# A two-layer graph kernel on one core: the first layer's product re-associated as A (x W0), its adjacency sums run in eight column passes, and each tile's norm and projections placed inside later tiles' sums

## The reference, cut to what matters

```python
# layer 0
a_hat = adjacency + eye;  dinv = rsqrt(deg)              # deg = max(row count of adj, 1)
a_norm = dinv * a_hat * dinv                             # [4096,1] factors: both scale rows
x1 = layernorm(x + relu((a_norm @ x + x) @ W0 + b0))
# layer 1, on x1
attn_a = sigmoid(concat[adj @ x1, x1] @ Wa.T + ba);      attn_b likewise with Wb, bb
h = x1 @ W_sa;  s_left = h @ a_l;  s_right = h @ a_r
e = where(adj != 0, exp(-leaky_relu(s_left[:, None] + s_right[None, :], 0.01)), 0)
x_a = (e / (e.sum(1) + 1e-5)) @ h
x_b = adj @ (x1 @ W_gcnb) + b_gcnb
out = layernorm(x1 + sigmoid(attn_a * x_a + attn_b * x_b))
```

## Time and profile before

| | |
|---|---|
| three runs | 918.81 us median, 917.81 to 919.22 |
| profiled execution, its span | 917.2 us, first to last instruction |
| PE busy, modelled | 887.0 us, 97% |
| DVE, ACT, POOL busy | 640.8, 461.9, 49.3 us |
| transfers | 121.49 MB, 132 GB/s over the span |

### The profile page before, as it was taken

One profiled execution on the slowest core, in us unless ns is written; L12 is line 12 of the kernel. 1 busy time (PEld: TensorE's weight loads), 2 busy tenths in 40 slices (PEclk: granted clock), 3 DMA queues, 4 the chain that ended last, 5 costly groups with the idle time before them and its releaser, 6 DMA issues.

```text
span 917.2 us, 18143 instructions
## 1 busy us (share of the span) xinstructions
PE 887.0 (97%) x6815; PEld 676.6 (74%) x6815; DVE 640.8 (70%) x1347; ACT 461.9 (50%) x652; POOL 49.3 (5%) x106
## 2 busy tenths in 40 slices
PE   3999999999999999997999999999999999999996
PEld 2444444444688788886888888888888888888885
DVE  5988810021599988869978768777786797797762
ACT  2400026665399966634745545554554564465350
POOL 0000000010122310000000000000000000000000
PEclk9999999999999999998999999999999999999998
DMA  9999959998613211020211110120120120110000
GB/s 337 422 416 416 417 210 396 330 388 339 253 47 128 75 36 53 1 75 13 75 65 31 56 63 17 58 74 11 63 74 11 63 74 11 63 54 32 13 24 12
DMA packets 44701, 121.49 MB, mean 132 GB/s; under 512 B 5456, under 2 KB 33136, under 8 KB 33520
## 3 DMA queue, kind: packets, MB, share of 16 engines
q1 hardware_dynamic: 44656, 120.89, 34.7%
HBM read 95.69 MB, written 25.18 MB: 132 GB/s over the span
## 4 chain that ended last, share of the span: by engine, by line
PE 77%; DVE 15%; issue 4%; ACT 3%; DMA 1%; POOL 0%; DVEq 0%; SPq 0%; POOLq 0%; ACTq 0%
PE ps L1067 33%; PE ps L924 24%; PE ps L1016 19%; DVE ec L788 3%; DVE ps L712 1%; DVE em L797 1%; DVE xs L717 1%; DVE fb L686 1%; DMA xs<-in_x_dram 1%; ACT ec L487 1%; DVE lnst L724 1%; DVE x1t L693 1%; ACT em L490 1%; DVE acct L675 1%; DVE sc L566 1%
## 5 line engine op out<-in xcount | busy, mean ns | idle before, releaser
L1067 PE MATMUL ps<-fb,em 128*128 128x257 f16 x3072 | 345.3, 275 | 6.4 <-DVE em L797 6.4
L1067 PEld LDWEIGHTS ps<-fb,em 128*128 128x128 f16 x3072 | 300.8, 98 | 48.7 <-issue 6.9
L1016 PE MATMUL ps<-fa,pan 128*128 128x258 f16 x2048 | 231.9, 273 | 0.0
L924 PE MATMUL ps<-res,y 128*128 128x512 fp8e4 x1024 | 222.0, 379 | 1.5 <-DVE y L633 0.8
L1016 PEld LDWEIGHTS ps<-fa,pan 128*128 128x128 fp8e4 x2048 | 199.3, 97 | 29.6
L788 DVE SCALAR_TENSOR_TENSOR ec<-slb,sr,pan 128x256 f32<-128x256 f32 x512 | 207.9, 479 | 7.7 <-issue 7.5
L487 ACT ACTIVATE ec<-ec,sc 128x2048 f32<-128x2048 f32 x64 | 127.9, 1999 | 133.6 <-DVE ec L788 133.6
L924 PEld LDWEIGHTS ps<-res,y 128*128 128x128 f16 x1024 | 100.0, 98 | 121.7 <-issue 1.2
L797 DVE SCALAR_TENSOR_TENSOR em<-ec,em 128x2048 f16<-128x2048 f32 x64 | 146.4, 2288 | 16.9 <-ACT em L490 16.9
L490 ACT ACTIVATE em<-ec 128x2048 f16<-128x2048 f32 x64 | 122.3, 1911 | 7.5
L414 ACT ACTIVATE res<-strip 128x2048 uint8<-128x2048 f32 x32 | 61.1, 1913 | 106.2 <-DMA strip<-in_adj_dram 106.2
(11 more groups left out here) (103 smaller groups left out, 477.6 us busy)
## 6 DMA issues: line engine op xcount, KB each, us to landing
strip<-in_adj_dram SPq DMA_DIRECT2D x63, 1024.0 KB, 9.8
a_scratch<-res SPq DMA_DIRECT2D x16, 1024.0 KB, 12.0
pan<-a_scratch SPq DMA_DIRECT2D x16, 1024.0 KB, 5.0
x_scratch<-xs SPq DMA_DIRECT2D x32, 128.0 KB, 1.7
x1r<-x_scratch SPq DMA_DIRECT2D x32, 128.0 KB, 2.1
out_dram<-ot SPq DMA_DIRECT2D x32, 128.0 KB, 1.7
xs<-in_x_dram SPq DMA_DIRECT2D x3, 1024.0 KB, 8.4
slb<-sl_scratch SPq DMA_DIRECT2D x16, 128.0 KB, 4.7
```

What stands on the lines that cost most here:

```text
L924: return pe.matmul(ps[:, sum_bank(g, dh), :], y[:, jb, part, dh * P:(dh + 1) * P], res[:, 2 * (g % NG2):2 * (g % NG2) + 2, jb, :].bitcast(F8),
L1016: mm = pe.matmul(PA(m)[:, 0:GC], pan[:, slot, jb, (m % 2) * P:(m % 2 + 1) * P].bitcast(F8), fa[:, jb, part, :], start=(jb == 0 and part == 0),
L1067: mm = pe.matmul(PH(m)[:, 0:HC], em[slot][:, e_part, jb, (m % 2) * P:(m % 2 + 1) * P], fb[:, jb, h_part, :], start=(jb == 0 and e_part + h ...
```

## The change

Layer 0 is `A (x W0)` in place of `(A x) W0`. By tile, in the order of the program:

- A first loop transposes each x tile on PE (`xt_step`), copies it out on ACT, multiplies it by W0 (`z_step`) and copies the result to `zf` on DVE (L613). `y` is now made of `zf`; its scale comes from a bound, the maximum of x times the largest absolute column sum of W0 (`z_bound`, `z_scale`). A column of ones in y gives the row count.
- The adjacency is read in 128 strips of four row tiles x 256 columns (1 KB contiguous in DRAM), ring of six, and cast by DVE (L600, a plain tensor_scalar) and ACT in turns, without accumulators. A pass covers two panels, q and q + 8, that is four row tiles (`PT = 4`). Codes of three passes are held in SBUF; each pass's codes go to DRAM when cast.
- `sum_rows` (L1031): the codes are stationary, 257 columns of y move, the result is untransposed, one bank a tile, and no bank is copied out. W0 is already in it.
- The first pass's rows are interleaved with the x W0 loop, 12 tiles behind. From the fifth tile on, a tile's 64 matmuls are cut in four quarters; after the first and third come `t_step` and `p_step` of the tile two before.
- DVE's per-tile work (`degree`, `residual`, `stats`, together `head`), ACT's normalize and copies, POOL's power and a new POOL add (z + bias, `zb`) follow. PE may not start tile n before the statistics of tile n - 4 are done (bank reuse).
- x1 goes to DRAM from ACT's queue, through a ring of four. The remaining steps, projections, A and E tiles, epilogue, are as before; panels are taken in the order q, q + 8.

```diff
-            for jb in range(T):
-                act.activation(y[:, jb, 0, :], xs[:, jb, :], ACT.Copy, scale=sc[:, SX]).then_inc(S["yhi_ready"], 1)
...
-            def sums(jb, dh, part, g):
-                return pe.matmul(ps[:, sum_bank(g, dh), :], y[:, jb, part, dh * P:(dh + 1) * P],
-                                 res[:, 2 * (g % NG2):2 * (g % NG2) + 2, jb, :].bitcast(F8),
...
+            z_bound()
+            for c in range(4):
+                x_max(c)
+            for t in range(T):
+                z_copy(t)
+                if t in (1, 3):
+                    x_max(4 + t // 2)
+                if t == 4:
...
+                if t == 5:
+                    z_scale()
+                if t >= YLAG:
+                    y_lo(t - YLAG)
+                if 9 <= t < 25 and t % 2 == 1:
+                    cast(1)
+                if t == 22:
+                    weight_columns()
+                if t == 26:
+                    weight_norm()
+                if t == 30:
+                    weight_scale()
+            for t in range(T - YLAG, T):
+                y_lo(t)
...
+            cast(6)
+            for n in range(3):
+                head(n)
+            cast(2)
...
+                sp.dma_start(strip[:, s % RING], adj_view[:, g * SJ:(g + 1) * SJ, c0:c0 + PW]
+                             ).then_inc(strip_in[s % RING], 16)
...
+                        mm = pe.matmul(ACC(n), codes[:, qq % SLOTS, h, jb, e * P:(e + 1) * P].bitcast(F8),
+                                       y[:, jb, part, :], start=(jb == 0 and part == 0),
+                                       stop=(jb == T - 1 and part == 1))
...
+            for t in range(T + 1):
+                if t < T:
+                    xt_step(t)
+                if t >= 1:
+                    z_step(t - 1)
+                if t - 1 >= ZLAG:
+                    pass0_rows(t - 1 - ZLAG)
...
+            def sum_tile(n, between):
+
+                if n >= PT:
+                    pe.wait_ge(S["stat_ready"], n - PT + 1)
+                for i in range(4):
+                    sum_rows(n, i * T // 4, (i + 1) * T // 4)
+                    for step, j in between.get(i, ()):
+                        step(j)
...
+                if n == PT:
+                    between = {0: ((t_step, 0),), 1: ((p_step, 0), (t_step, 1)), 2: ((p_step, 1),)}
+                elif n == PT + 1:
+                    between = {0: ((t_step, 2),), 1: ((p_step, 2), (t_step, 3)), 2: ((p_step, 3),)}
+                else:
+                    between = {0: ((t_step, n - 2),), 2: ((p_step, n - 2),)}
...
-            last_sums(5, 0)
-            last_sums(4, 0)
-            z_step(0)
+            pe.wait_ge(panel_in[0], 16)
+            pe.wait_ge(S["glo_ready"], T - 4)
+            pe.wait_ge(S["stat_ready"], T - 3)
+            a_rows(0, 0, 0, 8)
+            t_step(T - 2)
+            a_rows(0, 0, 8, 20)
+            p_step(T - 2)
+            a_rows(0, 0, 20, 28)
+            t_step(T - 1)
+            pe.wait_ge(S["glo_ready"], T - 3)
+            a_rows(0, 0, 28, 29)
+            pe.wait_ge(S["stat_ready"], T - 2)
+            a_rows(1, 0, 0, 10)
+            p_step(T - 1)
```

More of the change, by code:

```diff
@@ L447, in proj_copies, with cast @@
-            def proj_copies(t):
-                act.wait_ge(S["proj_done"], t + 1)
-                act.activation(q[:, t:t + 1], ps[:, BG(t), GC + 3:WG], ACT.Exp, scale=sc[:, QSC], bias=sc[:, QB]
+            todo = iter(ACT_CASTS)
+            def cast(count):
+                for s in [next(todo) for _ in range(count)]:
+                    cast_waits(act, s)
+                    act.activation(codes_of(s), strip[:, s % RING], ACT.Copy, scale=float(EDGE - NONE),
+                                   bias=float(NONE)).then_inc(S["cast_act"], 1)
@@ L1015, in a_rows @@
+            def a_rows(b, slot, j0, j1):
+                for j in range(j0, j1):
+                    jb = TILES[j]
                     for part in range(2):
[L1016 to L1022 removed]
```

996 lines of the change are left out of this document (508 added, 488 removed).

## The result

| | before | after |
|---|---|---|
| median of four runs | 918.53 us (917.81 to 919.22) | 944.61 us (942.95 to 945.49) |
| ratio, 95% interval | | 1.0282 (1.0267 to 1.0296) |
| profiled execution, span | 917.2 | 942.3, mean granted clock 0.983 |
| first sums | 20.28 | 29.13 |
| first relu chunk of layer 1 | 336.13 | 363.45 |

The changed kernel is 2.8% slower. The forecast was 943.8 us, and 942.2 for the span. The profiled execution took 944.09 us, 1.8 above its span.

What follows compares the result with a forecast made beforehand. PE was taken as the bound in layer 0, DVE and ACT from first relu chunk to third panel, then PE. The chunk coming 25.0 us later made 917.2 into 942.2, plus 1.6 is 943.8 us; range 924 to 968.

Steps and rivals of the forecast that it cites:

- The projections cost PE the same wherever they stand: Layer 0: putting projections inside the sums saves nothing by itself; they cost PE 1.34 + 0.23 us a tile.
- The sums, +5.8 us: Layer 0: 2048 matmuls of 257 columns at 0.111 take 227.3 us, against 221.5 before; 2 us more at most.
- The start, 29: Before the first sums: PE's products wait for DVE's copies behind maxima, plus 2 us slow clock; first sums at 29 us.
- The first pass, end at 84.8: First pass: DVE waits 10.75 us for POOL's power, so PE waits 6.4 us for low parts and ends at 84.8.
- The seam, 6.6 us to 91.4: After the first pass: six DVE casts and the first head hold PE's tile 4 for 6.6 us, until 91.4.
- Projection waits in tiles 4 and 5, 8.3 us: Behind the seam: PE waits 3.6 and 3.4 us in tile 4, 1.3 in tile 5; together 8.3, bounds 0 and 16.
- 8.68 us a tile: Remaining passes: 64 sums, projections and transposes take PE 8.68 us a tile, and nothing waits.
- Rival 2: The strips' transfers bound the passes if below 302 GB/s; at 250 GB/s the time is 994 us; chance 12%.
- Last sum 345.9, first relu chunk 361.1: End of layer 0: sums end at 345.9 us; layer 1's first relu chunk at 361.1, 25 us later than before.
- From relu chunk to the third panel 94.4, and 486.7 after: Layer 1: DVE and ACT's chain takes 94.4 us to the third panel, then PE runs 486.7 to the end, as before.
- Rival 1: The seams close: waits of 6.4 + 6.6 + 8.3 = 21.3 us go, time about 922 us; chance 20%, in parts.
- Rival 3: Faster: PE is fed from 5 us on and waits nowhere else in layer 0; 912.6 us; chance 7%.

Runs made afterwards that it cites:

- e7: Changed kernel reading each strip as 4 KB pieces from one row a partition instead of 1 KB from each of four rows; 943.56 us.
- e5: Changed kernel with layer-1 weights earlier, twelve second-pass casts moved into the x W0 loop, and first projection's copies ahead of head 3's normalization; 933.91 us.
- e1: Changed kernel with the six maxima of x, and DVE's waits for x's transfers, replaced by a constant 6.0; 943.39 us.
- the first three repairs: Each alone on the changed kernel: maxima of x made constant, 943.39 us; layer-1 weights earlier, 941.79; heads moved between the seam's casts, 943.09.

## Why the prediction was right, step by step

The total was right to 1 us and the sign for the reason given: PE has the same work as before or more, and the new order adds waits ahead of the first relu chunk. By its steps:

- **The projections cost PE the same wherever they stand.** Right: 1.33 us from 346.00 to 347.33, and 0.21 for the transposes, against 1.34 and 0.23 counted.
- **The sums, +5.8 us.** Under-sized. 0.1123 us each instead of 0.111, so 230.0 us and +8.5. The forecast had named 2 us as the most this could be off; it was 2.7. Layer 1's A tiles, with the same kind of stationary operand, kept 0.112, which was the nearer row. What the byte codes cost against f16 no run separates.
- **The start, 29.** 29.13, but by another path. The forecast has PE wait for DVE at product 2 (from 12.6 us) and again at product 6, behind the last maximum, and adds 2 us of slow clock. In the rows product 2 starts at 14.14, as the fourth part of x landed later than counted (DVE's maximum of it started at 11.38, not 10.3), and nothing waits after it: the three products at the slow clock cost some 0.9 us each more, and in their shade the two last maxima cost PE nothing (DVE itself waited 1.43 us for a product at 18.36). The sum is right because later x and slower products stand where the later waits were counted; this is luck. The clock was back at 20.25. The rule weighed beside it, that a loop of short bursts could stay slow, did not show.
- **The first pass, end at 84.8.** 83.64 (91.46 - 7.82). The term that was mis-sized is POOL's: DVE had the norm at 60.85 (counted 58.7) and the scale's first step at 68.16, 7.3 us and not the 10.75 of the earlier trace rows. PE also took the low parts as they came, and waited 1.67 and 1.11 us instead of 6.4 in one piece; all in all 4.9 us are lost in the pass, with 1.13 and 0.44 earlier in the loop.
- **The seam, 6.6 us to 91.4.** 7.82 to 91.46. Right in mechanism, and the later half to the tenth. DVE's rows of after show the casts and the end of the first head:

```profile
76.14 1.89 DVE L600 TENSOR_SCALAR codes<-strip 128x1024 uint8<-128x1024 f32 x3
80.96 0.69 DVE L600 TENSOR_SCALAR codes<-strip 128x1024 uint8<-128x1024 f32 x1 [2.94 <-DMA strip<-in_adj_dram]
85.18 0.69 DVE L600 TENSOR_SCALAR codes<-strip 128x1024 uint8<-128x1024 f32 x1 [3.53 <-DMA strip<-in_adj_dram]
88.19 0.69 DVE L600 TENSOR_SCALAR codes<-strip 128x1024 uint8<-128x1024 f32 x1 [2.31 <-DMA strip<-in_adj_dram]
...
91.25 0.15 DVE L766 TENSOR_SCALAR lnst<-lnst 128x1 f32<-128x1 f32 x1
```

  Casts to 88.8 (counted 88.7), then the head of 2.6 us (counted 2.7). DVE's first late strip was there at 80.96 (counted 81.9) and its next ones 4.2 and 3.0 us later (counted 3.0 each), so the tenth is two small errors that cancel.
- **Projection waits in tiles 4 and 5, 8.3 us.** 5.9, and the cause named was only half of it. DVE did wait, but for ACT, not behind its own casts:

```profile
98.09 0.60 ACT L450 ACTIVATE x<-x,lnst 128x256 f32<-128x256 f32 x1 [2.55 <-POOL lnst L380]
...
98.60 1.98 ACT L421 ACTIVATE codes<-strip 128x1024 uint8<-128x1024 f32 x2
100.49 0.36 ACT L459 ACTIVATE x1t<-ps 128x256 f16<-128x256 f32 x1
```

  These are ACT's rows. It normalized the third tile and made two casts before the copy that DVE's low part (100.88, waiting 3.22 us) and PE's projection need. The forecast had worked through DVE's program here and not ACT's. And it named the slow clock behind the seam (PE there after 5.8 us instead of 3.8) but gave it no term in the sum, though its own row at 430.55 showed one after a shorter wait; it cost 4.0 us. The two errors, 2.4 too much and 4.0 too little, partly cancelled.
- **8.68 us a tile.** 8.74 (337.26 to 346.00), no waits, as said. Rival 2 needed less than 302 GB/s; 324 were moved, and e7 took its ground away.
- **Last sum 345.9, first relu chunk 361.1.** 349.1 and 363.45. The 3.2 us are the clock's 4.0, 28 tiles x 0.06 = 1.7, and 2.4 less of waits. From last sum to relu chunk it was 14.3 instead of 15.2.
- **From relu chunk to the third panel 94.4, and 486.7 after.** 93.9 and 484.9. The forecast carried the old slow clock along; with a wait of 1.64 us it did not come. That gave back the 2 us by which layer 0 came out too long, so the total is right partly by luck: too much in the first pass and at the projections, too little for the sums and for the clock at the seam, and this clock, cancel to 0.1 us of span.
- **Rival 1** (the seams close, 922): e5 closed them and came to 933.9, as other waits opened. **Rival 3**: e1 shows it out of reach while the first strip comes behind all of x.

## What to carry to other kernels

Before believing that work is hidden "inside" other work, ask whether the host engine had idle time there; PE had none, and the new order only put waits in front of it. Where several in-order engines hand a tile on, removing one wait moved the next one forward: the first three repairs were worth 1.2, 2.8 and 1.5 us at the end, of which only the 2.8 is clear of the spread of the runs, and only the rearrangement of both queues at once (e5) gave 10.7. Read every engine's program at a seam, and charge the slow clock on top of a wait where a row of the same kernel shows one behind a wait as long. The version to keep is the old order with one extra power on POOL, 912.5 us.
